# One core: maxima of two heads in one instruction, and two in place of three banks for the shifted scores

## The reference, cut to what matters

```python
q = latents @ w_q.T                      # latents: layer-normed x, [32, 112, 256]
k, v = jnp.split(x @ w_kv.T, 2, axis=-1) # x: the context, [32, 375, 256]
attn = jnp.einsum('blhd,bshd->bhls', q, k) * SCALE      # 16 heads
attn = jax.nn.softmax(attn, axis=-1)
out = jnp.einsum('bhls,bshd->blhd', attn, v)
...
return out @ w_out.T + b_out
```

## Time and profile before

| | us |
|---|---|
| median of 3 runs | 1241.8 (1239.08 to 1242.07) |
| the profiled execution's own time | 1241.97 |
| its span, first to last instruction | 1240.2 |
| TensorE busy | 1072.6 (86%) |
| VectorE busy | 874.3 (70%) |
| ScalarE busy | 530.4 (43%) |
| GpSimd busy | 514.5 (41%) |

### The profile page before, as it was taken

One profiled execution on the slowest core, in us unless ns is written; L12 is line 12 of the kernel. 1 busy time (PEld: TensorE's weight loads), 2 busy tenths in 40 slices (PEclk: granted clock), 3 DMA queues, 4 the chain that ended last, 5 costly groups with the idle time before them and its releaser, 6 DMA issues.

```text
span 1240.2 us, 30762 instructions
## 1 busy us (share of the span) xinstructions
PE 1072.6 (86%) x9231; PEld 774.4 (62%) x9234; DVE 874.3 (70%) x2318; ACT 530.4 (43%) x953; POOL 514.5 (41%) x879
## 2 busy tenths in 40 slices
PE   7689999999999698989896589999999999766665
PEld 6567777777777466665553256666666666544444
DVE  4655666656655467676757678889888888578886
ACT  3312232233322111111114355666666665668885
POOL 1235444444443212222212134455544555566664
PEclk8879999999999799999999789999999999969998
DMA  9613333222332000000005687767767675630000
GB/s 227 167 49 94 93 92 87 85 84 86 92 93 81 19 1 0 0 0 0 1 1 115 136 175 155 156 153 160 154 150 160 152 160 126 205 128 25 25 25 30
DMA packets 121106, 116.08 MB, mean 94 GB/s; under 512 B 44867, under 2 KB 114022, under 8 KB 121062
## 3 DMA queue, kind: packets, MB, share of 16 engines
q1 hardware_dynamic: 119430, 115.20, 37.5%
q10 hardware_dynamic: 1632, 0.34, 0.1%
HBM read 79.15 MB, written 36.00 MB: 93 GB/s over the span
## 4 chain that ended last, share of the span: by engine, by line
PE 50%; DVE 25%; issue 11%; ACT 5%; SPq 3%; POOL 3%; DMA 2%; DVEq 1%; POOLq 0%; ACTq 0%
PE bank L1561 26%; DVE nm L1326 8%; PE bank L1719 6%; PE bank L1655 3%; PE bank L1845 2%; DVE hT L1258 2%; PE bank L1923 2%; PE bank L1644 2%; DVE yn L1247 2%; PE bank L1831 1%; ACT v_all L1054 1%; PE bank L1802 1%; POOL rs L731 1%; ACT v_all L1049 1%; DVE v_all L1446 1%
## 5 line engine op out<-in xcount | busy, mean ns | idle before, releaser
L1326 DVE TENSOR_REDUCE nm<-bank 112x1 f32<-112x375 f32 x512 | 247.2, 536 | 9.7 <-PE bank L1802 9.0
L985 ACT ACTIVATE pT<-bank 125x448 f32<-125x448 f32 x384 | 186.9, 543 | 90.8 <-PE bank L1831 88.5
L1802 PE MATMUL bank<-ks,qs 96*128 96x375 bf16 x512 | 164.0, 333 | 15.7 <-DVE nm L1326 13.4
L1831 PE MATMUL bank<-qs,ks 128*128 128x112 bf16 x1536 | 137.8, 214 | 5.3 <-DMA qs<-mrow 5.3
L1831 PEld LDWEIGHTS bank<-qs,ks 128*128 128x128 bf16 x1536 | 111.9, 99 | 26.7 <-DMA qs<-mrow 4.2
L1845 PE MATMUL bank<-pT,vaug 125*32 125x112 f32 x3072 | 101.1, 264 | 0.6 <-ACT pT L985 0.5
L936 ACT ACTIVATE yT<-bank,bcol,gcol 128x448 f32<-128x448 f32 x48 | 32.2, 721 | 160.4 <-PE bank L1701 160.4
L1719 PE MATMUL bank<-wffT,hT 128*112 128x256 f32 x384 | 99.2, 392 | 0.0
L1561 PE MATMUL bank<-wv1T,ctxT 128*125 128x256 f32 x384 | 88.0, 379 | 0.0
L1561 PE MATMUL bank<-ctxT,wk1T 128*128 128x375 f32 x256 | 86.6, 480 | 0.0
L1845 PEld LDWEIGHTS bank<-pT,vaug 125*32 125x32 f32 x3072 | 69.6, 110 | 25.0 <-issue 16.5
(11 more groups left out here) (206 smaller groups left out, 2314.6 us busy)
## 6 DMA issues: line engine op xcount, KB each, us to landing
k_parts_dram<-kp SPq DMA_DIRECT2D x192, 93.8 KB, 3.5
ks<-k_parts_dram SPq DMA_DIRECT2D x64, 281.2 KB, 4.2
cnat<-in_ctx_dram SPq DMA_DIRECT2D x32, 375.0 KB
ks<-k_parts_dram SPq DMA_DIRECT2D x64, 187.5 KB, 4.2
ks<-k_parts_dram SPq DMA_DIRECT2D x64, 93.8 KB, 3.9
q_parts_dram<-qp SPq DMA_DIRECT2D x48, 112.0 KB, 2.2
qs<-q_parts_dram SPq DMA_DIRECT2D x64, 84.0 KB, 3.4
x_stream<-in_x_dram SPq DMA_DIRECT2D x4, 896.0 KB, 13.1
```

The lines of the kernel that those rows point to most:

```text
L985: act.activation(pT[:, u % 6, :], B3[u % 3][0:TP], ACT.Exp).then_inc(probs_made, 1)
L1326: dve.tensor_reduce(nm[:, h:h + 1], scores[0:L], AX_X, ALU.max, negate=True).then_inc(head_max_taken, 1)
L1802: mm(A3[h % 2 if first else h % 3], qs[par][0:KS, h * L:h * L + P], ks[par][0:KS, h * T:(h + 1) * T], start=True, stop=True).then_inc(max_ ...
L1831: last = mm(B3[c][:, j * L:(j + 1) * L], ks[par][:, h * T + c * TP:h * T + c * TP + P], qs[par][:, h * L:(h + 1) * L], start=True, stop=True)
```

## The change

Two heads' maxima are taken by one instruction. A pair of heads p gets two neighbouring banks (A3 now has two sides of two banks, 6-7 and 4-5), TensorE fills both, and VectorE reads both with one reduction of 112 rows by 2 by 375 into two columns of `nm`. The semaphores count pairs. Pair p of a batch uses side p mod 2 and waits for pair p - 2 to be taken. For the first batch, pairs 0, 1 and 2 are made during the query steps of the stage before, all on side 0, and pair 3 waits until the last query product has left banks 4 and 5. The four banks come from B3, which keeps two of its three banks, so `scores` of unit u now waits for the exponential of unit u - 2. PV3 moves from bank 4 to bank 2. The small steps on VectorE are put behind the same number of heads, or one head away.

```diff
-    AHEAD = 10
+    AHEAD = 5
...
-        A3 = [bank[:, i, 0:T] for i in (6, 7, 5)]
-        B3 = [bank[:, i, 0:4 * L] for i in range(3)]
-        PV3 = bank[:, 4, 0:HQ * L].rearrange("p (g l) -> p g l", g=HQ)
+
+        A3 = [bank[:, i:i + 2, 0:T] for i in (6, 4)]
+        B3 = [bank[:, i, 0:4 * L] for i in range(2)]
+        PV3 = bank[:, 2, 0:HQ * L].rearrange("p (g l) -> p g l", g=HQ)
...
-        FIRST = [()] * (NG - 3) + [(0, 1), (2, 3), (4, 5)]
+        FIRST = [()] * (NG - 3) + [(0,), (1,), (2,)]
+        FIRST_P = FIRST[-1][-1] + 1
+
+        def side_of(b, p):
+
+            return 0 if isinstance(b, int) and b == 0 and p < FIRST_P else p % 2
...
-                act.activation(pT[:, u % 6, :], B3[u % 3][0:TP], ACT.Exp).then_inc(probs_made, 1)
+                act.activation(pT[:, u % 6, :], B3[u % 2][0:TP], ACT.Exp).then_inc(probs_made, 1)
...
-            def maxima(b, h):
-                scores = A3[h % 2] if isinstance(b, int) and b == 0 else A3[h % 3]
-                dve.wait_ge(max_scores_made, 16 * b + h + 1)
-                dve.tensor_reduce(nm[:, h:h + 1], scores[0:L], AX_X, ALU.max, negate=True).then_inc(head_max_taken, 1)
+            def maxima(b, p):
+                dve.wait_ge(max_scores_made, H8 * b + p + 1)
+                dve.tensor_reduce(nm[:, 2 * p:2 * p + 2], A3[side_of(b, p)][0:L], AX_X, ALU.max,
+                                  negate=True).then_inc(pair_max_taken, 1)
...
-                for k in range(H):
-                    if k < H - AHEAD:
+                for k in range(H8):
+                    if k < H8 - AHEAD:
                         if not isinstance(b, int) or b < B - 1:
                             maxima(b + 1, k + AHEAD)
                     elif not isinstance(b, int) or b < B - 2:
-                        maxima(b + 2, k - (H - AHEAD))
-                    if later and k == 1:
+                        maxima(b + 2, k - (H8 - AHEAD))
+                    if later and k == 0:
                         norm_o(b - 1)
+                    if later and k == H8 - AHEAD - 1:
+                        x4(b - 1)
+                    if k == H8 - AHEAD - 1 and (not isinstance(b, int) or b < B - 1):
+                        parts_m(b + 1)
+                    if later and k == 4:
+                        stats4(b - 1)
                     if later and k == 5:
-                        x4(b - 1)
-                    if later and k == 10:
-                        stats4(b - 1)
-                    if later and k == 11:
                         aggregate4(b - 1)
-                    if later and k == 12:
+                    if later and k == 6:
                         keep4(b - 1)
-                    if k == H - AHEAD - 1 and (not isinstance(b, int) or b < B - 1):
-                        parts_m(b + 1)
...
-                if first and h >= 2:
-                    pe.wait_ge(head_max_taken, h - 1)
-                elif not first and h >= 3:
-                    pe.wait_ge(head_max_taken, 16 * b + h - 2)
-                elif not first:
-                    pe.wait_ge(head_max_taken, 16 * b)
-                mm(A3[h % 2 if first else h % 3], qs[par][0:KS, h * L:h * L + P], ks[par][0:KS, h * T:(h + 1) * T],
-                   start=True, stop=True).then_inc(max_scores_made, 1)
+                p = h // 2
+                if h % 2 == 0:
+                    if first and p < FIRST_P:
+                        if p >= 1:
+                            pe.wait_ge(pair_max_taken, p)
+                    elif first and p == FIRST_P:
+
+                        pe.wait_ge(q_rest_part3_made, 2 * NG - 1)
+                    else:
+                        pe.wait_ge(pair_max_taken, H8 * b + p - 1)
+                made = mm(A3[side_of(b, p)][:, h % 2], qs[par][0:KS, h * L:h * L + P], ks[par][0:KS, h * T:(h + 1) * T],
+                          start=True, stop=True)
+                if h % 2:
+                    made.then_inc(max_scores_made, 1)
...
-                if not isinstance(b, int) or 12 * b + u >= 3:
-                    pe.wait_ge(probs_made, 12 * b + u - 2)
+                if not isinstance(b, int) or 12 * b + u >= 2:
+                    pe.wait_ge(probs_made, 12 * b + u - 1)
...
-                    last = mm(B3[c][:, j * L:(j + 1) * L], ks[par][:, h * T + c * TP:h * T + c * TP + P],
+                    last = mm(B3[u % 2][:, j * L:(j + 1) * L], ks[par][:, h * T + c * TP:h * T + c * TP + P],
                               qs[par][:, h * L:(h + 1) * L], start=True, stop=True)
```

More of the change, by code:

```diff
@@ L338, in xattn_ffn_kernel @@
         half_in = [[sem(f"{n}_heads_in{i}") for i in range(3)] for n in ("low", "high")]
-        (ones_rows_made, max_scores_made, head_max_taken, minus_max_steps, minus_max_parts_made,
+        (ones_rows_made, max_scores_made, pair_max_taken, minus_max_steps, minus_max_parts_made,
          minus_max_turned, minus_max_rows_ready, minus_max_in_place, shifted_scores_made,
@@ L343, in xattn_ffn_kernel @@
          v_laid_out, x_plus_bout_made, pads_zeroed, ffn2_row_factor_steps) = sems(
-            "ones_rows_made max_scores_made head_max_taken minus_max_steps minus_max_parts_made "
+            "ones_rows_made max_scores_made pair_max_taken minus_max_steps minus_max_parts_made "
             "minus_max_turned minus_max_rows_ready minus_max_in_place shifted_scores_made probs_made "
@@ L1331, in query_step @@
                     normed(e + 2, s)
-                for h in FIRST[e]:
-                    maxima(0, h)
+                for p in FIRST[e]:
+                    maxima(0, p)
                 q_rest(e, s)
@@ L1338, in _ @@
                 query_step(e, e % 2)
-            for h in range(FIRST[-1][-1] + 1, H):
-                maxima(0, h)
+            for p in range(FIRST[-1][-1] + 1, H8):
+                maxima(0, p)
             stage_end(dve, "dve", 3)
             def parts_m(b):
-                dve.wait_ge(head_max_taken, 16 * b + 16)
+                dve.wait_ge(pair_max_taken, H8 * b + H8)
                 dve.tensor_copy(npart[:, 0:H], nm[:, :]).then_inc(minus_max_steps, 1)
@@ L1388, in step3 @@
                 if isinstance(b, int) and b == 0:
-                    for h in range(H):
-                        maxima(1, h)
+                    for p in range(H8):
+                        maxima(1, p)
                     parts_m(1)
-                    for h in range(AHEAD):
-                        maxima(2, h)
+                    for p in range(AHEAD):
+                        maxima(2, p)
                     return
-                for k in range(H):
-                    if k < H - AHEAD:
+                for k in range(H8):
+                    if k < H8 - AHEAD:
                         if not isinstance(b, int) or b < B - 1:
@@ L1807, in query_step @@
                     rows_turn(e + 1, 1 - s)
-                for h in FIRST[e]:
-                    scores_for_max(0, 0, 0, h)
+                for p in FIRST[e]:
+                    for h in (2 * p, 2 * p + 1):
+                        scores_for_max(0, 0, 0, h)
                 query(e, s)
@@ L1812, in _ @@
                 query_step(e, e % 2)
-            for h in range(FIRST[-1][-1] + 1, H):
+            for h in range(2 * FIRST_P, H):
                 scores_for_max(0, 0, 0, h)
@@ L1872, in step3 @@
                 later = not isinstance(b, int) or b >= 1
-                heads = [(b + 1, (par + 1) % 3, n + (par == 2), h) for h in range(AHEAD, H)]
+                heads = [(b + 1, (par + 1) % 3, n + (par == 2), h) for h in range(2 * AHEAD, H)]
                 if isinstance(b, int) and b == B - 1:
@@ L1876, in step3 @@
                 if not isinstance(b, int) or b < B - 2:
-                    heads += [(b + 2, (par + 2) % 3, n + (par >= 1), h) for h in range(AHEAD)]
+                    heads += [(b + 2, (par + 2) % 3, n + (par >= 1), h) for h in range(2 * AHEAD)]
                 at_once = 1
                 if isinstance(b, int) and b == 0:
-                    heads = [(1, 1, 0, h) for h in range(AHEAD)] + heads
+                    heads = [(1, 1, 0, h) for h in range(2 * AHEAD)] + heads
                     at_once = 2
@@ L1946, in _ @@
             fin_rows(B - 1)
-            pe.wait_ge(head_max_taken, 16 * B)
+            pe.wait_ge(pair_max_taken, H8 * B)
             pe.wait_ge(probs_made, 12 * B)
```

## The result

The changed kernel takes 1285.02 us (median of 4 runs, 1283.64 to 1286.12); the kernel before took 1241.93 us (4 runs, 1239.08 to 1243.16) beside it. The ratio is 1.035, with a 95% interval of 1.033 to 1.0371. Slower was forecast, at 1280.0 us, with 1264 to 1292 as the range.

What follows compares the result with a forecast made beforehand. VectorE's leg was taken to set the second attention's period, with TensorE having some slack. From 1241.97 us, +37.1 (period), -1.1 (start), +0.4 (batch 0) and +1.7 (last batches) gave 1280.1, forecast as 1280, range 1264 to 1292.

Steps and rivals of the forecast that it cites:

- The mechanism and the period: Second attention: S11 waits for exponential 9 behind m_out and mrow's DMA issue; period 11.17 to 12.45 us, +37.1 over 29 intervals.
- The sign that was 0.3 us of waiting at S8: Profile after: TensorE at `scores` waits 0.3 us for ScalarE's exponential at S8.
- The pair's pitch: VectorE's reductions: a pair of heads takes 0.85 us from one start to the next, bounds 0.79 to 0.91.
- A saving of 0.36 us in the leg: VectorE from x4 to `on`: pairing the 12 heads there saves 0.06 us a pair, 0.36 in all.
- The walk: One batch followed across the engines' queues from x4, through S8, m_out, exponential 9 and S11, to the next x4 at 12.45.
- the saving of 0.75 us in the leg: VectorE's leg: the page's fixed PSUM cost would save 0.125 us a pair, 0.75 in all; the forecast noted pitch 0.455 disagrees.
- The start: Stage's start: batch 0's last ten reductions, 5.55 us, become five pairs, 4.33; -1.1 us (0 to -1.2).
- forecast 0.4: Batch 0: S2 and S3 wait for the first exponentials, +0.4 us, bounds 0 and +1.
- The end: Batches 30 and 31: the wait behind m_out moves weigh(9-11) by 1.1 and 0.6 us; +1.7 (0.8 to 2.5).
- VectorE's pace: Rival: VectorE sets the period and new waits hide in TensorE's slack; 1230 us, chance 0.04.
- Break-even: Rival: half of S11's hold is absorbed, shorter reductions pay for the rest; 1242 us, chance 0.03.
- The clock falls: Rival: TensorE, less busy in each period, is granted a mean clock of 0.90; 20 us more, 1300, chance 0.06.

Runs made afterwards that it cites:

- the one with two copies more: Changed kernel with two added ScalarE copies of 512 elements behind the DMA issue of mrow, in front of exponential 9: 1357.64 us, ratio 1.0917.
- the kernel before with three DMAs: The kernel before with the DMA of mrow cut in three parts, one for each bf16 part: 1336.18 us, ratio 1.0774.
- after, three DMAs: The changed kernel with the DMA of mrow cut in three parts, one for each bf16 part: 1345.08 us, ratio 1.0835.

## Why the prediction was right, and where its sum was off

**The mechanism and the period: right.** Step by step, counted from x4, forecast and measured: S8 0.68 and 0.69; m_out 2.22 and 2.23; exponential 9 3.46 and 3.48; S11 4.05 and 4.08; pair 2 4.62 and 4.65; M of head 9 6.59 and 6.62; fin_turn 9.41 and 9.46; x4 12.45 and 12.49. The 29 intervals give +38.2 us (12.484 - 11.166 = 1.318 each), forecast +37.1. The experiments show the cause and do not merely agree with it: without the DMA in front, 0.96 of the 1.32 go; with the chain moved up by the 0.7 of a weigh, 0.67 go; with 0.93 more in it, 0.92 come on top. The sign that was 0.3 us of waiting at S8 shows in the weight load alone (0.39).

**The pair's pitch: right in the sum, and smaller in effect than its own sentence said.** 0.85 was taken; two in a row take 1.78, so the pitch is 1.78 - 0.94 = 0.84, and one takes 0.936 (forecast 0.93). A saving of 0.36 us in the leg was named; with VectorE waiting for pairs anyway it comes to 0.19 in a whole batch (1289.09 against 1285.02), and the arrangement in pairs takes away more than that. The walk held this, since it let pair 2 wait for its second head; the sentence on what a pair saves did not. Of a fixed part for each PSUM read, the Trainium skill ("VectorE: DVE Perf Modes", the TRN2 errata) would make 120 cycles at 0.96 GHz: by it 0.906 for the 750 elements, near the 0.936 here, but 0.516 as the time from one single head to the next, where rows 3 show 0.455. The page fits the duration of one instruction and not the pitch of several, and the saving of 0.75 us in the leg that followed from it did not appear.

**The start: wrong sign.** Forecast -1.1. The last five reductions of batch 0 took the 0.93 us less that the step counts on:

```profile
704.09 4.62 DVE L1332 TENSOR_REDUCE nm<-bank 112x2 f32<-112x750 f32 x5
```

But the first `parts_m` came 1.2 us later than before. In front of it the query products of the stage before had been slower (8 matmuls at 684.98 us took 5.23 us, 3.67 before), at a lower granted clock (0.60 over them, 0.86 before). The first x4 of the profiled kernels lies anywhere from 734.6 to 739.2 us, with no relation to their edits; the step was right by its rows and is smaller than this scatter. Batch 0 then took 1.5 us more, forecast 0.4; 0.5 of it lies ahead of S0, between `parts_m` and the landing of `mrow`'s DMA (6.16 us, 5.65 before), where no term of the forecast stood.

**The end: mis-sized.** +1.7 was forecast for the last two batches and +4.85 measured (22.42 against 17.57). The rule "m_out's wait moves weigh(9-11)" explains its share: with the load out of the way the two intervals are 10.27 + 9.32 = 19.6, +2.0. The other 2.8 are `mrow`'s DMA beside the load of L585. The forecast took that DMA to be as it was; the change moved it from 0.54 us ahead of a large load to 0.24 ahead. Behind the last x4 the changed kernel took 1.6 us less (161.1 against 162.7; the other kernels took 159.0 to 162.6), for which I have no experiment.

Together: 38.2 + 1.2 + 1.5 + 4.85 - 1.6 = 44.1, the difference of the spans.

**The rivals.** VectorE's pace (1230) asked for a hold under the slack: measured 1.69 at S11, so it fell. Break-even fell with it. "The clock falls" (1300) did not happen in the 29 intervals, at 1.00 with waits of 1.25 us; with waits of 2.16 us in the experiment it did, to 0.86. The Trainium skill ("TensorE: Matmul & The Clock Gate", the second failure mode) names such short idle times between groups as what makes a kernel lose the clock repeatedly. The changed kernel's stage does not bear this out, the one with two copies more does. The forecast's own ground for a small chance, single gaps of under 2 us, was not enough: the kernel before with three DMAs lost clock (0.88) with gaps of 1.0 to 1.6 us.

**Left open.** Why `mrow`'s DMA lands 2 to 3 us later beside that load is not settled: which of the DMA engines or queues it waits in was not tried. What makes the clock fall is open too, and the length of one wait in each batch does not settle it: 1.25 us goes with 1.00 in the changed kernel, 1.0 to 1.6 us with 0.88 (before, three DMAs), 2.16 with 0.86 (after, copies) and 2.30 with 0.94 (after, three DMAs).

## What to carry to other kernels

A spare bank is worth what it hides: before taking one away, walk the queue of the engine that frees it, DMA issues included, and see which item stands in front of the one that will now be waited for. Two operations in one instruction save only the part that does not overlap already, and they make the reader wait for both inputs; in a stream with short waits the second can cost more than the first gives. When a change shifts a stage by fractions of a microsecond, look at what large transfer its small DMAs now stand next to.

## What the hardware showed that I had not expected

- A small DMA (10.5 KB) issued within 0.26 us of a load of 896 KB on another queue was waited for until 4.9 to 6.0 us after its issue; 0.54 us ahead of the load, its reader ran 2.63 us after the issue without a wait.
- TensorE's granted clock held 1.00 over 350 us at 84% busy with one wait of 1.25 us a batch, and fell to 0.86 with one of 2.16 us. The fall then cost more (1.66 us a batch) than the lengthening of the wait (0.92). In two other kernels it was 0.88 with waits of 1.0 to 1.6 us and 0.94 with waits of 2.30, so a longer wait need not mean a lower clock.
- A VectorE copy of 112x2 numbers took 0.70 us in place of 0.17 beside a GpSimd addition, and ended with it. The Trainium skill ("SBUF — State Buffer", "SBUF: two separate sides") says that GpSimd and VectorE instructions of certain forms share a pair of ports as an exclusive lock, so that the one that comes second blocks fully; the two ends 0.01 us apart, and the copy that started 0.04 us behind the addition, agree. No run here changes the copy's form, so none shows that it is one of these forms.
- With a DMA issue between them on ScalarE's queue, the next activation started 1.25 us behind the start of the copy in front, and 0.16 us behind it without; the issue itself is recorded as 0.73 us.
